# A third PSUM bank for the experts' first layer, taken from the normalised tokens' transposes

## What is computed

```
def _expert_stack(x, W1, b1, W2, b2):
    h = gelu(einsum('btd,edf->ebtf', x, W1) + b1)
    return einsum('ebtf,efd->ebtd', h, W2) + b2
shared_enc = _expert_stack(x, sW1, sb1, sW2, sb2).sum(0)       # 128 -> 512 -> 128
weights = softmax(x @ gW + gb)                                 # 15 experts
topv, topi = top_k(weights, 3)
gated = (one_hot(topi, 15) * topv[..., None]).sum(-2)
router_out = _expert_stack(x, rW1, rb1, rW2, rb2)              # each 128 -> 256 -> 128
router_enc = einsum('ebtd,bte->btd', router_out, gated)
return shared_enc + router_enc + x
```

## Time and profile before

| | us |
|---|---|
| median of 3 runs | 2109.78 (2108.49 to 2114.78) |
| the profiled execution, its own time | 2105.3 |
| its span, first to last instruction | 2103.5 |
| first expert matmul of tile 0 to last second-layer matmul | 402.3 to 851.6 |
| one tile's turn, from the same instruction to the next | 54.7 |

### The profile page before, as it was taken

How to read it: one execution, slowest core, us unless ns; L and a number is a source line. 1 busy time by engine, 2 the same in 40 slices (tenths; PEclk the granted TensorE clock), 3 DMA queues, 4 the chain that set the end, 5 groups by cost and what they waited for, 6 DMA issues and landing times. The chain is left out here.

```text
span 2103.5 us, 62415 instructions
## 1 busy us (share of the span) xinstructions
PE 1865.1 (89%) x23360; PEld 1476.1 (70%) x23422; DVE 1459.6 (69%) x3889; ACT 1447.1 (69%) x4195; POOL 1118.4 (53%) x1445
## 2 busy tenths in 40 slices
PE   5799788399999999699859999867999999999898
PEld 3566556277777777466648888745888888888787
DVE  7699748466666665477746676667777777777567
ACT  5588657388888888488848888746666666666542
POOL 5567437388888889455423333228444444545520
PEclk9999969699999999799989999998999999999999
DMA  3100000432222222000011111120000000000101
GB/s 87 36 25 25 12 8 3 97 91 71 73 72 73 70 73 76 12 2 2 2 42 32 32 32 32 27 69 4 5 15 17 3 18 5 15 15 3 55 8 38
DMA packets 60908, 72.51 MB, mean 34 GB/s; under 512 B 10553, under 2 KB 38985, under 8 KB 60353
## 3 DMA queue, kind: packets, MB, share of 16 engines
q1 hardware_dynamic: 51392, 64.32, 10.4%
q10 hardware_dynamic: 9216, 4.20, 0.7%
HBM read 51.46 MB, written 4.44 MB: 27 GB/s over the span
## 5 line engine op out<-in xcount | busy, mean ns | idle before, releaser
L1037 POOL TENSOR_TENSOR ff_hl<-ff_hid,ff_hh 128x512 fp32r<-128x512 f32 x272 | 351.3, 1307 | 89.4 <-ACT ff_hh L1280 81.8
L1897 POOL TENSOR_TENSOR sm_zsum<-sm_zsum,sm_logits 128x512 f32<-128x512 f32 x120 | 154.6, 1288 | 273.2 <-ACT sm_logits L1923 271.5
L1201 DVE TENSOR_TENSOR ff_hid<-ff_p_b,ff_gates 128x512 f32<-128x512 f32 x240 | 164.8, 687 | 151.9 <-ACT ff_p_b L1269 151.2
L1940 ACT ACTIVATE sm_sT<-sm_p_s 128x512 f32<-128x512 f32 x128 | 69.5, 595 | 219.3 <-PE sm_p_s L1733 219.3
L594 ACT ACTIVATE at_pr<-at_p_s,at_small 128x64 f32<-128x64 f32 x512 | 154.9, 329 | 60.4 <-DVE at_small L480 60.4
L1280 ACT ACTIVATE ff_hh<-ff_hid 128x512 fp32r<-128x512 f32 x272 | 169.9, 625 | 35.5 <-DVE ff_hid L1201 35.5
L1269 ACT ACTIVATE ff_p_b<-ff_p_h,ff_b 128x512 f32<-128x512 f32 x240 | 157.1, 655 | 20.7 <-PE ff_p_h L1100 19.6
L1909 POOL TENSOR_TENSOR sm_logits<-sm_logits,sm_peak 128x512 f32<-128x512 f32 x128 | 163.0, 1295 | 12.5 <-ACT sm_comb L1958 11.9
L1747 PE MATMUL sm_p_l<-g_phi,g_xnT 128*128 128x256 f32 x512 | 142.3, 404 | 26.5 <-ACT sm_logits L1968 25.4
L561 POOL TENSOR_TENSOR at_kblk<-at_kT,at_heads 128x512 f32<-128x512 f32 x128 | 131.7, 1049 | 37.8 <-PE at_p_s L459 26.4
L1098 PE MATMUL ff_p_h<-ff_xh,ff_w1h 128*128 128x512 f32 x272 | 113.8, 418 | 25.2 <-ACT ff_hid L1269 11.5
(11 more groups left out here) (297 smaller groups left out, 5603.2 us busy)
## 6 DMA issues: line engine op xcount, KB each, us to landing
ff_gates<-kept_gates SPq DMA_DIRECT2D x120, 256.0 KB, 3.1
xa_kturn<-xa_ksin SPq DMA_DIRECT2D x128, 64.0 KB, 2.0
at_turned<-at_terms SPq DMA_DIRECT2D x64, 64.0 KB, 1.9
sm_w<-in_w_soft SPq DMA_DIRECT2D x8, 512.0 KB, 3.4
ff_whole<-in_L_ffn_rW SPq DMA_DIRECT2D x30, 128.0 KB, 3.6
early_xs<-in_x ACTq DMA_DIRECT2D x32, 64.0 KB, 1.9
ld_ctx<-in_ctx ACTq DMA_DIRECT2D x32, 64.0 KB, 2.1
x_kept<-early_xs SPq DMA_DIRECT2D x1, 2048.0 KB, 7.4
```

The lines of the kernel that those rows point to most:

```text
L1037: eng.tensor_tensor(hl[:, q, :], hid[:, q, :], hh[:, q, :].bitcast(F32), ALU.subtract).then_inc(h_split, 1)
L1201: dve.tensor_tensor(h, p_b[c % 2][:, :], gates[:, n % GR, :], ALU.mult).then_inc(scaled, 1)
L1897: pool.tensor_tensor(z, z, logits[:, j % RING_L, :, :], ALU.add).then_inc(summed, 1)
```

## The change

`PH` goes from 2 to 3, so the first layer's results go through three banks in turn. The bank for it comes from `p_n`: the normalised tokens' transposes now go to columns 0 to 127 of `p_q`, the router's bank. Since `p_q` now has three uses in a turn (logits, the four transposed blocks, the transposed `sel`), PE gets two more waits: ahead of the first transposed block, for the DVE step that has read the logits (or, in the last turns, for the copy of the gates); and ahead of the transposes of `sel` at c = 21, for ACT's copies of all four transposed blocks.

```
-    GR, PH = 5, 2
+    GR, PH = 5, 3
...
-        p_y, p_t, p_n, p_q = m.ps("p_y"), m.ps("p_t"), m.ps("p_n"), m.ps("p_q")
+        p_y, p_t, p_q = m.ps("p_y"), m.ps("p_t"), m.ps("p_q")
...
                     if c == AT_G_T and nxt:
                         pe.wait_ge(r_step, STEPS * (t + 2))
+                        if old:
+                            pe.wait_ge(norm.copied, 4 * t)
                         for q in range(4):
                             mm = pe.transpose(p_q[0:NE, q * P:(q + 1) * P], sel[:, q, :], g["ident"][:, :])
...
-                        pe.transpose(p_n[:, 0:P], norm.xn[:, q % 2, :], g["ident"][:, :]).then_inc(norm.transposed, 1)
+                        if q == 0:
+
+                            if nxt:
+                                pe.wait_ge(r_step, STEPS * (t + 1) + 1)
+                            else:
+                                pe.wait_ge(gT_copied, min(t + 1, NGR))
+                        pe.transpose(p_q[:, 0:P], norm.xn[:, q % 2, :], g["ident"][:, :]).then_inc(norm.transposed, 1)
...
-                        norm.act_copy(act, 4 * (t - 1) + AT_LNT.index(c), p_n[:, 0:P])
+                        norm.act_copy(act, 4 * (t - 1) + AT_LNT.index(c), p_q[:, 0:P])
```

## The result

| | before | changed |
|---|---|---|
| median, us | 2110.66 (20 runs, 2106.35 to 2116.13) | 2116.47 (20 runs, 2112.27 to 2119.63) |
| profiled execution: span | 2103.5 | 2117.4 |
| first expert matmul to last normalised block's transpose | 402.3 to 860.2 | 402.6 to 865.4 |
| one tile's turn (from one transpose of `sel` to the next) | 54.71 | 55.49 |

The ratio of changed to before is 1.0021, with a 95% interval of 1.0014 to 1.0029: the change makes the kernel 0.2% slower, some 4.4 us (3.0 to 6.1), within the 0.3% that was set as the bound, and not by chance. The two medians lie 5.8 us apart, inside that interval too. Forecast were +0.19% and 2113.8 us; the median of 2116.47 is 2.7 us over that, 0.9 us of it because the median before is now that of 20 runs and not of three.

A forecast was written before the change was run, and what follows sets the result against it. PE was taken to bound the kernel, busy 89% of the span. The new wait's +4.3 us and turn 0's -0.3 us gave +4.0 us, so 2109.78 becomes 2113.8 us; forecast range 2110 to 2118, wider range 2105.0 to 2119.0.

The forecast's parts named there:

- What bounds a middle turn: Experts' middle turns: PE bounds them apart from its gaps, busy 51.57 of 54 us; from step 13 to 21 DVE does.
- The bank wait of a middle turn: Step 10: the 1.11 us gelu wait goes, 0.3 us is left at step 11, 0 from step 13, behind POOL and DVE.
- Rivals 1 and 2: Bank wait gains 7.8 us in full: new wait hidden, 2102.0 us (chance 0.08); new wait counted too, 2106.3 us (0.12).
- The new wait: Step 21, turns 1 to 6: `sel`'s transposes wait for ACT's fourth copy, 0.71 us a turn, +4.3 us in all.
- rival 3: Behind step 21 an unseen slack makes up PE's 0.71 us; only turn 0's 0.3 us stay: 2109.5 us; chance 0.12.
- Turn 0: First turn of the experts: bank waits mostly move one step later to ACT's and POOL's delays; -0.3 us stays.
- a rival for the middle turns: Longer stop at step 21 pulls PE's clock down, some 1.6 us lost six times: 2123.7 us; chance 0.08.
- The total: Whole kernel: +4.3 - 0.3 = +4.0 us, 0.19% more, likeliest verdict within 0.3% on the slow side.
- The rule for the change: Skill's rule: consistent bubbles on the busiest engine can mean too little SBUF or PSUM; the third bank would give -7.8 us.

The follow-up runs named there:

- e3: The changed kernel with the transposes of `sel` at step 22 instead of 21: 54.31 us a turn, ratio 0.9998 to the kernel before.
- e2: The kernel before, with two banks, with the transposes of `sel` at step 22 instead of 21: 54.33 us a turn, ratio 0.9999 to the kernel before.
- e4: The changed kernel with the fourth normalised block at step 21 instead of 20 and `sel` at 23 instead of 21: 54.67 us a turn, ratio 0.9997.
- e1: The changed kernel with PH back at 2, shared bank and its two waits kept: 55.51 us a turn, ratio 1.0029 to the kernel before.
- g1: f3 with the normalised blocks at steps 15, 17, 19, 21 and `sel` at 24: 53.32 us a turn, ratio 0.9940 to the kernel before.
- g2: Kernel before, two banks, with lag 5, gate ring 4, normalised blocks at steps 15, 17, 19, 21, `sel` at 24: 54.74 us a turn, ratio 0.9988.
- f3: Changed kernel with lag 5 instead of 4, hidden ring 5, gate ring 4, fourth block at step 21, `sel` at 23: 54.11 us a turn, ratio 0.9961.

## Why the prediction was right

- **What bounds a middle turn.** Right for the steps and the lag of the kernel before. PE sets the pace outside steps 8 to 21, and in these steps DVE's row does, through ACT and POOL. e3 against e2 shows that a wait of PE ahead of that stretch's end costs nothing. e4 fits it: two of PE's waits went, and a third one came in their place.
- **The bank wait of a middle turn, worth 0.** Right, to 0.02 us a turn in e2 and e3. The steps were as worked out: step 10 without a wait, step 11 stopped by POOL, no difference at step 13. Rivals 1 and 2, which paid the 7.8 us in full, fall with it.
- **The new wait, 0.71 us x 6.** Right in kind, place and number of times; 0.78 us a turn was measured (55.49 - 54.71), so 4.7 us instead of 4.3. The difference is the delay with which PE follows the copy: 0.14 us after its row's end, where I had taken the 0.05 to 0.06 us of the other two. e1 shows that the whole of it belongs to the shared bank. Nothing behind step 21 makes it up, so rival 3 falls: the six turns are 4.7 us longer, and the experts 4.9.
- **Turn 0, worth -0.3 us.** Not confirmed, and in the profile of the wrong sign. From the first expert matmul to `sel`'s transposes it took 453.27 - 402.62 = 50.65 us, before 452.79 - 402.33 = 50.46: +0.2 instead of -0.3. What failed is the step that let PE reach step 11 early enough. PE did run one step ahead (a stop of 7.7 us for the gelu instead of 11.1, of 1.9 instead of 3.9), but stood 1.5 us for POOL at 430.5 and then ran for longer at the lower clock. The busy times by 2 us before:

```profile
430.00:432.00 2.00, 2.00 (x6) 1.57 (x5) 1.58 (x5) 2.00 (x4) 1.81 (x3) 0.50 0.11 36
432.00:434.00 2.00, 2.00 (x8) 1.61 (x8) 0.69 (x1) 1.98 (x3) 2.00 (x2) 0.80 0.41 101
434.00:436.00 2.00, 1.36 (x6) 0.78 (x5) 0.22 (x1) 1.96 (x4) 0.40 (x1) 1.00 0.54 125
```

and in the changed kernel:

```profile
430.00:432.00 2.00, 1.49 (x4) 1.20 (x5) 1.60 (x5) 2.00 (x4) 1.79 (x3) 0.50 0.09 33
432.00:434.00 2.00, 2.00 (x6) 1.60 (x5) 0.71 (x2) 1.98 (x3) 2.00 (x2) 0.50 0.38 103
434.00:436.00 2.00, 2.00 (x6) 1.52 (x5) 0.21 (x1) 1.96 (x4) 0.43 (x1) 0.50 0.36 126
```

  The clock of 0.50 (1.2 of 2.4 GHz) lasts to about 436.7 us instead of 432.8, so step 10 began at 436.91, where it had begun at 436.33, and was not ahead any more. I had the fall of the clock in a rival for the middle turns, but not in this term. That the third bank brings this on is not shown: in e2, with two banks, the clock is at 0.50 for as long (427.2 to 434.0 us). Nor is the term itself large enough to be seen. Step 20 of turn 0 begins 47.74, 48.00 and 48.02 us after the first expert matmul in the kernels with two banks and a lag of four (before, e1, e2), and 47.93, 47.74 and 47.88 us in those with three (changed, e3, e4). That turn scatters by as much as the 0.3 us, and what the bank is worth in it at this lag stays open.
- **The clock in the middle turns.** The rival fell: the granted clock of turn 3 stayed 1.00 (588 to 643 us) with a stop of 1.05 us at step 21, and it did so from 436.7 us to the end of the last turn.
- **The total.** +4.0 forecast, +4.4 by the ratio, +4.9 in the experts of the profiled execution. The two misses, +0.4 for the wait and +0.5 for turn 0, have the same sign and add up to what the profile shows over the forecast. The wait's is a matter of size; turn 0's lies within that turn's scatter, so there the sum came out close without being tested.
- **The rule for the change.** The Trainium skill, Perfetto Trace Analysis, section Optimization Strategy (it stands there, right behind the section that the prediction names), has it that consistent bubbles can mean too little PSUM. Here the bubble was a wait for a bank, and its removal gave 0 at a lag of 4 and 1.42 us a turn at a lag of 5 with later steps (g1 against g2).

## What to carry to other kernels

A wait that the profile names is worth only what the next wait leaves of it: walk the bounded engine on to the next two places where it waits, and see whether their releasers depend on it. In this kernel a buffer more helped only where the other things that the same engine waits for were at least that far ahead, so the number of buffers, the lag between the layers and the places of the small jobs belong together (0, 0.48 and 1.42 us a turn for the same bank; a longer lag with e3's steps gave nothing). When two uses are put into one bank, look where the last reader stands in its own engine's queue: here one step later for the next writer made the sharing free.

## What was not expected

PE followed its releases at two distances. Where the instruction's record in the trace has one semaphore to wait for, it was 0.05 to 0.06 us behind the end of the row that gave it, for a gelu, POOL's low part and DVE's steps alike, in all eleven profiles. For `sel` behind ACT's copy the record has two semaphores, and it was 0.14 us, six times each in the changed kernel, e1 and f3; the same 0.14 us stand in g1 between the copies and the next block's transpose, which has two semaphores there. In g1 six of these transposes wait last for DVE, with 0.12 us, where f3 has 0.06 us for the same pair of instructions with one semaphore. So the longer distance goes with the second semaphore. No run was made for this alone, and these kernels differ in their steps too.

Two attention stages that no kernel here touched differed by up to 7 us between executions, together with the granted clock (0.97 to 0.95). For changes of 0.2% the sum over one profile is of no use, while the repeated turn tells 0.1 us.
